# Moving row puts, the owners and the list reading, and splitting the load semaphores, in a fused scan and mixture-of-experts kernel

## The reference

```python
x = x + attn(layernorm(x), w_qkva, gamma)      # x: 4 x 1024 x 256, float32
x = x + ffn(layernorm(x), router_w, w_gate, w_up, w_down, sw_gate, sw_up, sw_down)

# attn: h = rmsnorm(x) * gamma; q, kv, a = split(h @ w_qkva.T); a = sigmoid(a)
#       y_t = a_t * y_(t-1) + kv_t along the sequence; returns q * y

# ffn, on the 4096 rows as x_flat:
logits = x_flat @ router_w.T                   # 7 experts
top_vals, top_idx = jax.lax.top_k(logits, 2)
top_w = jax.nn.softmax(top_vals, axis=-1)
combine = jnp.sum(jax.nn.one_hot(top_idx, 7) * top_w[..., None], axis=1)
# swiglu: (silu(x @ w_gate) * (x @ w_up)) @ w_down, 256 -> 1024 -> 256
mixed = jnp.einsum('end,ne->nd', swiglu(x_flat, routed experts), combine)
mixed = mixed + jnp.mean(swiglu(x_flat, shared expert), axis=0)
```

## Time and profile before

| | us |
|---|---|
| median of 3 timed runs | 1039.39 |
| profiled execution | 1041.65 |
| its span, first to last instruction | 1039.9 |
| PE busy | 1007.9 (97%) |
| DVE busy | 627.5 (60%) |
| ACT busy | 523.5 (50%) |
| POOL busy | 504.4 (49%) |

### The profile page before, as it was taken

The page is one execution under the profiler, slowest core; times in us unless marked ns, Lnnn a source line. Parts: engine busy times, 40 slices in busy tenths (PEclk is TensorE's granted clock), DMA queues, the critical chain, the costliest instruction groups (busy, mean ns, idle before and its releaser), DMA issues.

```text
span 1039.9 us, 19706 instructions
## 1 busy us (share of the span) xinstructions
PE 1007.9 (97%) x7277; PEld 950.3 (91%) x7277; DVE 627.5 (60%) x1095; ACT 523.5 (50%) x786; POOL 504.4 (49%) x283
## 2 busy tenths in 40 slices
PE   7999999999999796999999999999999999999998
PEld 5788999989999696999999999999999999999997
DVE  7987677787423143555556565656565655547776
ACT  4554433222212255666666666666666666653232
POOL 2236200000010367777877777777877787750000
PEclk9999999999999898999999999999999999999999
DMA  9333300012587727777777777777777777728341
GB/s 314 99 85 81 82 11 21 11 60 78 169 286 262 266 66 262 224 256 233 258 235 256 234 259 229 259 233 261 233 255 239 254 232 256 247 71 242 113 142 40
DMA packets 162029, 192.75 MB, mean 185 GB/s; under 512 B 76089, under 2 KB 147266, under 8 KB 151746
## 3 DMA queue, kind: packets, MB, share of 16 engines
q1 hardware_dynamic: 155248, 173.83, 51.7%
q0 software_dynamic: 6720, 18.36, 5.7%
q10 hardware_dynamic: 18, 0.01, 0.0%
HBM read 165.42 MB, written 26.74 MB: 185 GB/s over the span
## 4 chain that ended last, share of the span: by engine, by line
PE 76%; DVE 9%; DMA 8%; issue 3%; SPq 3%; ACT 1%; POOL 0%; DVEq 0%; POOLq 0%; ACTq 0%
PE ps L1012 46%; PE ps L1027 15%; PE ps L1031 7%; DMA sorted_rows<-x_stage 5%; PE ps L919 3%; DVE y_sb L1200 2%; PE ps L903 1%; PE ps L1053 1%; DMA w_first<-in_L_ffn_w_down_dram 1%; SPq L421 1%; DVE h_early L1516 1%; DVE hT_lo L1160 1%; PE ps L1060 1%; SPq L404 1%; DVE h_lo L1521 1%
## 5 line engine op out<-in xcount | busy, mean ns | idle before, releaser
L1012 PE MATMUL ps<-xs_hi,w_both 128*128 128x256 f32 x3072 | 566.9, 284 | 10.8 <-DVE ps L1516 8.9
L1012 PEld LDWEIGHTS ps<-xs_hi,w_both 128*128 128x128 f32 x3072 | 481.3, 190 | 13.8 <-DVE ps L1516 9.1
L1012 PE MATMUL ps<-xs_lo,w_both 128*128 128x256 f32 x1536 | 436.0, 284 | 0.0
L585 POOL TENSOR_TENSOR w_both<-raw,w_both 128x2048 fp32r<-128x2048 f32 x67 | 318.4, 4752 | 105.3 <-ACT w_both L745 97.0
L1012 PEld LDWEIGHTS ps<-xs_lo,w_both 128*128 128x128 f32 x1536 | 291.8, 190 | 0.1
L1027 PE MATMUL ps<-w_both,h_hi 128*128 128x512 f32 x768 | 273.6, 398 | 0.9 <-DVE h_lo L1521 0.7
L1031 PE MATMUL ps<-w_both,h_lo 128*128 128x256 f32 x768 | 215.5, 281 | 0.0
L784 ACT ACTIVATE silu<-ps 128x512 f32<-128x512 f32 x192 | 114.3, 595 | 199.8 <-PE ps L1012 199.8
L745 ACT ACTIVATE w_both<-raw 128x1024 fp32r<-128x1024 f32 x192 | 192.4, 1051 | 10.6 <-DMA raw<-in_L_ffn_w_up_dram 9.2
L1516 DVE TENSOR_TENSOR ps<-ps,silu 128x512 f32<-128x512 f32 x160 | 111.9, 699 | 133.0 <-ACT silu L784 126.7
L1027 PEld LDWEIGHTS ps<-w_both,h_hi 128*128 128x128 f32 x768 | 144.4, 188 | 35.0 <-DVE h_lo L1521 1.8
(11 more groups left out here) (192 smaller groups left out, 798.7 us busy)
## 6 DMA issues: line engine op xcount, KB each, us to landing
raw<-in_L_ffn_w_up_dram SPq DMA_DIRECT2D x33, 1024.0 KB, 5.3
raw<-in_L_ffn_w_gate_dram SPq DMA_DIRECT2D x33, 1024.0 KB, 8.6
raw<-in_L_ffn_w_down_dram SPq DMA_DIRECT2D x33, 1024.0 KB, 5.5
sorted_rows<-x_stage SPq DMA_DIRECT2D x32, 256.0 KB
x_rows<-sorted_rows SPq DMA_DIRECT2D x128, 64.0 KB, 5.3
got<-expert_rows SPq DMA_DIRECT2D x10, 512.0 KB, 6.1
z_rows<-z_all SPq DMA_DIRECT2D x8, 512.0 KB, 2.9
x_rows<-z_rows SPq DMA_DIRECT2D x64, 64.0 KB, 2.3
```

The source lines that it names most:

```text
L585: pool.tensor_tensor(w_lo[buf][:, k, :], source[:, k, :], w_hi[buf][:, k, :].bitcast(F32), ALU.subtract).then_inc(wlo_ready[k], 1)
L1012: last = pe.matmul(o, w[:, part, at[kd]:at[kd] + P], xx[:, u, kd, :], start=i == 0, stop=i == len(terms) - 1)
```

## The change

It does five things:

1. SP issues puts and row loads of several blocks ahead of the singles' weights: blocks 0 and 1 before the weights of single 0, puts 2 and 3 before those of single 1, put 5 before those of single 5, put 6 before w_first.
2. GpSimd gathers blocks 6 and 7 ahead of scatter 3, and these two gathers no longer wait for transposed rows; SP waits for that once ahead of its loop.
3. The down part of a single's weights has a semaphore of its own, and each part of w_first has one.
4. VectorE's owners move from the end of slot 5 to the end of slot 7; the positions of the second choice move from the end of slot 4 to the middle of slots 3 and 4.
5. The list reading is cut in two: `idx_x` signals `listed` at once, `idx_y` is made one pair later and signals it again.

```diff
-            def load_all(i, dst, signal):
+            def load_all(i, dst, signals):
                 sources = rows_of_expert(i)
                 for k in (1, 0, 2):
-                    sp.dma_start(parts_of(dst)[k], sources[k]).then_inc(signal, 16)
+                    sp.dma_start(parts_of(dst)[k], sources[k]).then_inc(signals[k], 16)
...
-                load_all(i, w_lone[i], lone_in[i])
+                load_all(i, w_lone[i], (lone_in[i], lone_in[i], lone_down_in[i]))
...
-            sp.wait_ge(routed, 1)
-            for k in range(3):
-                sp.wait_ge(wlo_ready[k], 1)
-            load_lone(0)
             sp.wait_ge(listed, 1)
             for i in range(2):
                 put_x(i)
                 load_sorted(i)
+            for k in range(3):
+                sp.wait_ge(wlo_ready[k], 1)
+            sp.wait_ge(routed, 1)
+            load_lone(0)
+            for i in range(2, 4):
+                put_x(i)
             load_lone(1)
-            put_x(2)
             load_sorted(2)
             load_lone(2)
             load_x(LATE, SA - 1, z_dram, LATE % 2)
-            for i in range(3, NS):
-                load_lone(i)
-                put_x(i)
-                load_sorted(i)
+            load_lone(3)
+            load_sorted(3)
+            put_x(4)
+            load_lone(4)
+            put_x(5)
+            load_sorted(4)
+            load_lone(5)
+            load_sorted(5)
+            put_x(NS)
             sp.wait_ge(down_psum, LATE + 2)
             load_all(NS, w_first, first_in)
-            put_x(NS)
             load_sorted(NS)
+            put_x(NS + 1)
             sp.wait_ge(down_psum, slot_of(3) + 2)
             load_expert(1, 1)
-            put_x(NS + 1)
+            sp.wait_ge(xT_psum, slot_of(NS + 1) + 1)
...
-                if i >= NS:
+                if i >= NS + 2:
                     pool.wait_ge(xT_psum, slot_of(i) + 1)
...
+            pool.wait_ge(listed, 2)
             for i in range(2):
                 scatter_y(i)
                 gather_x(i + 4)
-            for i in range(2, 4):
-                scatter_y(i)
+            scatter_y(2)
             gather_x(NS)
+            gather_x(NS + 1)
+            scatter_y(3)
             split_lo(0, 1, 0, w_first)
-            gather_x(NS + 1)
             scatter_y(4)
...
-                act.wait_ge(first_in, 48)
+                act.wait_ge(first_in[k], 16)
...
-                pe.wait_ge(lone_in[i], 48)
+                pe.wait_ge(lone_in[i], 32)
...
+                pe.wait_ge(lone_down_in[i], 16)
                 pe.wait_ge(down_free, n + 1)
...
+            for n in range(3, LISTED):
+                between = {0: lambda n=n: hot_rows(2 * (n - 3)), "down": lambda n=n: lists(n)}
+                if n == 3:
+                    between[2] = lambda: pick(1)
                 if n == 4:
-                    positions(1)
-                if n == 5:
-                    owners()
+                    between[2] = lambda: halves_of(1)
...
+            slot(n, n % 2, LD * (n // 2 + 1 + n % 2), shared=n, early=True, skip=0, between={
+                1: take_lists, 2: take_targets, "down": owners})
```

More of the change, by code:

```diff
@@ L227, in preln_scan_moe_kernel @@
         lone_in = [sem(f"lone_in{i}") for i in range(NS)]
-        first_in = sem("first_in")
+        lone_down_in = [sem(f"lone_down_in{i}") for i in range(NS)]
+        first_in = [sem(f"first_in{k}") for k in range(3)]
         consts = sem("consts")
@@ L1391, in shift, with pick, halves_of @@
                 step(dve.tensor_scalar(tmp[:, :, :], tmp[:, :, :], float(P * NS), None, ALU.add))
-            def positions(k):
+            def pick(k):
                 step(dve.tensor_tensor(first[:, k, :, :], first[:, k, :, :], tmp[:, :, :], ALU.mult))
                 step(dve.tensor_reduce(pos_f[:, :], first[:, k, :, :], AX_X, ALU.add))
+            def halves_of(k):
                 step(dve.tensor_scalar(pos_hi[:, k, :], pos_f[:, :], 1.0 / P, 0.5 / P - 0.5,
@@ L1466, in take_lists, with take_targets @@
                 step(dve.tensor_scalar(rows_f[:, 1, :], rows_f[:, 1, :], 0.0, None, ALU.max))
-                step(dve.tensor_copy(idx_x[:, :], rows_f[:, 1, :]))
+                dve.tensor_copy(idx_x[:, :], rows_f[:, 1, :]).then_inc(listed, 1)
+            def take_targets():
+                dve.wait_ge(listed, 1)
                 step(dve.tensor_scalar(rows_f[:, 1, :], count_f[:, 0:COLS], float(P), float(TOP * N + P),
@@ L1591, in rows_of_first @@
                 shift()
-                positions(0)
+                pick(0)
+                halves_of(0)
             slot(1, 1, 2 * LD, shared=1, early=True, skip=0, between={
@@ L1603, in lists @@
                 hot_cols(c + 1)
+            for n in range(3, LISTED):
+                between = {0: lambda n=n: hot_rows(2 * (n - 3)), "down": lambda n=n: lists(n)}
+                if n == 3:
+                    between[2] = lambda: pick(1)
                 if n == 4:
-                    positions(1)
-                if n == 5:
-                    owners()
-            for n in range(3, LISTED):
-                slot(n, n % 2, LD * (n // 2 + 1 + n % 2), shared=n, early=True, skip=0,
-                     between={0: lambda n=n: hot_rows(2 * (n - 3)), "down": lambda n=n: lists(n)})
+                    between[2] = lambda: halves_of(1)
+                slot(n, n % 2, LD * (n // 2 + 1 + n % 2), shared=n, early=True, skip=0, between=between)
             n = LISTED
-            slot(n, n % 2, LD * (n // 2 + 1 + n % 2), shared=n, early=True, skip=0, between={1: take_lists})
+            slot(n, n % 2, LD * (n // 2 + 1 + n % 2), shared=n, early=True, skip=0, between={
+                1: take_lists, 2: take_targets, "down": owners})
             n = FIRST_LONE - 1
```

## The result

The changed kernel takes 1028.31 us (median of 4 runs, 1027.55 to 1028.68), the kernel before, in the same comparison, 1039.7 (4 runs, 1038.4 to 1040.96). The ratio is 0.9892, with an interval of 0.9866 to 0.9917: 11.4 us faster. The forecast was 1027 us, range 1024 to 1032.

The account below looks back on a forecast made before the run. PE was taken as the bound, so only its waits count: 10.22 + 2.28 = 12.5 us off the profiled 1041.65 gives 1029.15; 2.26 lower for the median gives 1026.9, say 1027 us, range 1024 to 1032.

Parts of the forecast that it names:

- Stall A: PE's 7.02 us wait in slot 14, behind the late w_first load; claimed to go, -10.22 us.
- lower bound: Least gain in slot 14: with an unmoved queue, part semaphores alone leave 2.6 us of loss, gaining 7.6 us.
- Slots 5 and 6: VectorE's positions and owners delay its additions there; moving them was claimed to give -2.28 us.
- The additions in slots 3 and 4: Position instructions added to VectorE there, delaying it 0.9 and 0.8 us; claimed cost 0, far end +1.7 us.
- Slot 7: List reading cut in two, one half after the third pair, owners before the two additions; claimed cost 0.
- Single 0's weights: First single's weights, now queued behind puts, row loads and owners; claimed cost 0 with 2.3 us of cover.
- Rival 1: First single waits for its weights, 2 to 4 us late, costing 3 to 6 us: 1030 to 1033; chance 0.10.
- Stall B: PE's 8.9 us wait in slot 17, on a chain starting with slot 16; claimed change 0, bounds -1 to +1 us.
- Rival 3: The 8.9 us wait in slot 17 goes or shrinks too: 1018 or below; chance 0.04.
- Rival 2: Queue isn't free in time, only the part semaphores work, leaving 2.6 us in slot 14: 1029.5; chance 0.06.
- Rival 4: Slower: single 0's weights so late that slot 9's wait eats all, from 10.9 us of lateness; chance 0.04.
- The price of 1.46 per idle us: Cost of each idle us of PE, read from slot 14: 10.22 us lost for 7.02 idle.

Follow-up runs that it names:

- e3: Changed kernel, but ScalarE waits for all three parts of w_first before rounding the first: 1028.09 us, ratio 0.9883.
- e1: Kernel before with only a semaphore for each part of w_first, all queues keeping their order: 1033.45 us, ratio 0.9943.
- e1b: The kernel before with the part semaphores alone, profiled a second time: 1032.26 us (one run).
- e2: Changed kernel with VectorE's moves undone, positions back at the end of slot 4 and owners at the end of slot 5: 1030.6 us, ratio 0.9909.
- e9: Changed kernel with idx_y read behind the owners in slot 7, not after its third pair: 1027.09 us, ratio 0.9892.
- e7: Changed kernel with GpSimd's gather of block 8 ahead of its split of the gate part in slot 16: 1019.61 us, ratio 0.9802.
- e6: Changed kernel with single 0's weights held back until PE has made slot 8's down products: 1039.36 us, ratio 1.0005.
- e5: Changed kernel with single 0's weights held back until VectorE has made slot 8's last product: 1035.44 us, ratio 0.9964.
- e10: Changed kernel with the edits of e7 and e9 together: 1019.65 us, ratio 0.9802.
- e11: e10 with GpSimd's split of the down part in slot 16 held back until VectorE's split of the up part: 1024.98 us, ratio 0.9854.
- e8: e7's order and e9's idx_y, with ScalarE's rounding of the third raw load's gate and down parts moved later, into slot 17: 1021.3 us, ratio 0.983.

## Why the prediction was right

- *Stall A, -10.22 us.* Right to the hundredth: 20.82 to 10.60 us. The mechanism is right in both halves. The order alone ends it (e3), and the semaphores alone end most of it (e1). What the prediction called the lower bound, 7.6 us if nothing in the queue moved, was too high by medians: e1 gained 6.4. In e1b's profile the two singles lose 2.47 us, so 7.75 of stall A's 10.22 are gone, close to the 7.6, but by luck: I had priced ScalarE's wait (1.75 us) as PE's. ScalarE's 1.15 us cost PE 0.10, and the rest comes from the late `raw` load that stops PE in slot 15, a step that I hadn't followed beyond w_first. Why the medians show 1.3 us less, no trace tells. Between e1 and e2, which differ by the queue order and what goes with it, lie 2.85 us.
- *Slots 5 and 6, -2.28 us.* 2.31 in the profile, 2.3 by e2. The additions in slots 3 and 4, costed at 0, cost nothing: slots 4 to 6 all take 19.1.
- *Slot 7, 0.* 0.14 us shorter, and the cut list reading still cost it 0.56 us of waiting, which e9 took away. Too small to matter.
- *Single 0's weights, cost 0 with 2.3 us of cover.* No wait, and 4.3 us of cover. The issue came at 265.71, 1.8 us before the 267.5 that I took, and the part took 7.0 us for 7.9. Of the 1.8 us, 0.5 are the earlier start of this execution. Rival 1 fell. By the rule in the Trainium skill (SBUF — State Buffer, "SBUF: two separate sides") on descriptors that GpSimd can't write, each of the first two gathers would have lost 2.5 us (an estimate from the page). The trace shows no such loss: POOL's timeline after, beside the earlier trace rows,

```profile
253.29 1.30 POOL L620 DMA_INDIRECT x_stage<-z_rows,idx_x  x1 [126.43 <-DVE idx_x L1479]
254.89 1.03 POOL L620 DMA_INDIRECT x_stage<-z_rows,idx_x  x1 [0.30 <-issue]
```

  has the same 1.30 and 1.03 us, 4.1 us earlier. The first gather takes 1.30 us in all 13 profiles. Whether a two-port instruction of VectorE ran beside these two isn't shown, so the rule itself wasn't tested here.
- *Stall B, 0.* Its wait is 8.87 us after 8.92, and the third raw load is issued 378.60 - 358.07 = 20.5 us after slot 16 begins, and it was 20.6 in the kernel before. e7 moves one link of that chain and 8.7 us go. Rival 3 asked for what no step of the change does.
- *Rival 2.* w_first is issued 1.25 us after slot 12 (the forecast said within 1), so the queue was free in time.
- *Rival 4.* It didn't come, and its point was well placed. It said that the kernel is slower from 10.9 us of lateness on, of which 2.3 are cover: 8.6 us past the need. e6 has 8.63 us and takes as long as the kernel before. That the point fits so well is in part luck: the gain that it divides was 11.4 us by medians and not 12.5, and the price was 1.33 and not 1.46, and the two errors cancel.
- *The price of 1.46 per idle us.* Right for stall A, from which it was read, but no constant. Stall A lost 10.22 us for 7.02 idle, stall B 28.69 - 17.16 = 11.53 for 8.87, e5 6.96 for 4.39, e6 11.44 for 8.63: the idle time and 2.6 to 3.2 us more. The other profiles widen this to 1.6 to 3.2 us (see the last section). The ratio is 1.59 at 4.39 us and 1.33 at 8.63. At e6's 8.63 us the price of 1.46 gives 12.6, which is 1.2 too much.
- *The total.* The forecast of the profiled execution was 1029.15, and it took 1028.17. The 0.98 us are the start (0.48), slot 17 (0.32) and slot 7 (0.14), and 0.03 in slots 5 and 6. By medians I forecast 1026.9 and it was 1028.31, because I took the 2.26 us by which the profiled execution before stood above its median over to the changed kernel. There the two lie 0.14 us apart. The kernel before scatters over 7 us, e1 over 5, and after, e2, e3 and e9 over 2 at most. I read this as the time at which put 5 lets w_first go, which differs from run to run (335.70 and 338.16 in e1's two profiles). That isn't shown: executions without a trace can't show it, and e5, e6, e7 and e10, which have the new queue order too, scatter over 2.8 to 3.4 us. Two other sources stand in the profiles: slot 4 begins between 182.80 and 184.43, and slot 17, where stall B is untouched, takes 27.76 to 29.07 us. The 0.48 and 0.32 us above are smaller than these and so are no gain of the change.

## What to carry to other kernels

A wait in an in-order queue holds all behind it: look for the load that the stalled engine wants, and ask what it stands behind and not how long it takes. Then follow the loads behind it as well, since a part semaphore can pass the lateness on to the next. When weights lose cover, work out how late they may be, and a kernel that holds them back by that much shows whether the margin is real. One moved gather with its chain read to the end (e7, 8.7 us) was worth nearly as much as the five moves of the change.

## What the runs showed of the hardware

- *A long wait costs more than its length, by 1.6 to 3.2 us, and the amount doesn't grow with the wait.* PE waited 4.39 us in e5 and lost 6.96, 7.02 in stall A and lost 10.22, 7.46 in e11 and lost 27.50 - 17.16 = 10.34, 8.63 in e6 and lost 11.44. Stall B was waited for 8.87 to 9.34 us in nine profiles, and slot 17 lost 10.60 to 11.91. In all of them the granted clock fell to 0.50 while PE stood and stayed there for a while once it worked again. How long it stayed makes the difference. The changed kernel's stall B, where PE starts again at 390.52 and 2.66 us come on top of 8.87, in windows of 1 us (columns as above):

```profile
395.00:396.00 1.00, 1.00 (x6) 1.00 (x6) 0.31 (x1) 0.00 (x0) 0.98 (x2) 0.50 0.72 254
396.00:397.00 1.00, 1.00 (x11) 1.00 (x10) 0.32 (x1) 0.60 (x1) 1.00 (x1) 1.00 1.12 418
```

  And e9's, where PE starts again at 389.94 and 10.63 - 8.95 = 1.68 us come on top:

```profile
392.00:393.00 1.00, 1.00 (x7) 1.00 (x6) 0.68 (x1) 0.29 (x1) 0.84 (x2) 0.50 0.84 352
393.00:394.00 1.00, 1.00 (x10) 1.00 (x9) 0.66 (x2) 1.00 (x2) 0.88 (x1) 0.90 1.19 156
```

  PE worked 5.5 us at the low clock in the one and about 3.2 in the other, and half of that is what came on top.

  Short waits can go either way. At a granted clock of 1.00 throughout, e1b's 2.10 us made slot 15 longer by 2.37, and e8's 0.93 and 0.61 us made slot 17 longer by 2.21. But the 2.45 us of e7 and the 1.79 us of e10, each 3.1 us behind a wait of 0.93, were followed by a granted clock of 0.50 for 3 to 4 us: slot 17 lost 5.30 us for 3.38 of waiting and 4.72 for 2.72.
- *VectorE's split and GpSimd's don't run side by side.* In e7 VectorE's began at 376.44, inside GpSimd's of 374.59 to 379.22, and ended 1.08 us behind that; alone it takes 2.36 / 2 = 1.18. GpSimd's took its usual 4.63. So VectorE's wasn't slowed evenly: by these times nearly all of it was made after GpSimd had ended. The other way round, in the changed kernel, GpSimd's split began at 367.42, 0.39 us into one of VectorE that took its usual 1.22 us, and GpSimd's took 5.30 us. The one that starts first isn't held up.

  The Trainium skill says the same (SBUF — State Buffer, "Who interferes with whom"): a tensor_tensor of VectorE with both inputs in SBUF contends with GpSimd's reads, and the second one is blocked until the first has finished. The trace agrees. The page infers that such an instruction doesn't hinder GpSimd's descriptors. The traces of this case say otherwise. Nine gathers in six profiles (e1b, e2, e7, e8, e9, e10) began while VectorE's splits were running, and they took 1.80 to 2.07 us. The one of e9, in the timelines of DVE and POOL:

```profile
401.30 2.36 DVE L1517 TENSOR_TENSOR w_both<-raw,w_both 128x1024 fp32r<-128x1024 f32 x2 [1.20 <-ACT w_both L753]
```

```profile
401.36 2.07 POOL L620 DMA_INDIRECT x_stage<-z_rows,idx_x  x1 [0.30 <-issue]
```

  All other gathers, but for the first of each profile, took 1.01 to 1.07 us, also those that began about 0.4 us ahead of the splits and ran into them.
- *An issue can be slow.* The issue of four row loads of the shared expert took SP 8.24 us, right behind three parts of weights (SP's timeline of the changed kernel); the two groups of four ahead of the weights took 1.74. The same four took 4.64 to 4.97 us in the three profiles with the old queue order, and 8.19 to 9.04 in the ten with the new one.

```profile
282.07 0.38 SPq L405 DMA_DIRECT2D w_spare<-in_L_ffn_w_down_dram  x1
282.55 8.24 SPq L361 DMA_DIRECT2D x_rows<-z_rows  x4
291.55 0.71 SPq L405 DMA_DIRECT2D raw<-in_L_ffn_w_up_dram  x1
```

  Here it was covered. I had counted an issue by its position in the queue alone.
